# Expert rows added straight into the output, with filling rows written by scatter

## The reference, cut to what matters

```python
x = L0_attn_x                                  # (2, 1024, 512)
xn = _layernorm(x, axis=-1)
x = x + attention(xn, w_attn, b_attn, w_proj, b_proj) + experts(xn, gate_w, w1, w2)
# experts: top 2 of softmax(xn @ gate_w.T), weights divided by their sum
topw, sel = jax.lax.top_k(probs, TOP_K)
act = jax.nn.silu(g) * u                       # g, u: halves of x @ w1[e].T
out = jnp.einsum('eth,te->th', act @ w2[e].T, combine)
```

## Time and profile before

| | us |
|---|---|
| median of three runs | 886.06 |
| the profiled execution | 894.05 |
| its span, first to last instruction | 892.3 |
| PE, DVE, ACT, POOL busy | 809.3, 542.7, 400.9, 256.0 |
| `project_qkv`, up to the first instruction of the next block | 0 to 177.8 |
| `attend` | 177.8 to 553.75 |
| `experts` | 553.75 to 892.3 |

### The profile page before, as it was taken

The page is one execution under the profiler, slowest core; times in us unless marked ns, Lnnn a source line. Parts: engine busy times, 40 slices in busy tenths (PEclk is TensorE's granted clock), DMA queues, the critical chain, the costliest instruction groups (busy, mean ns, idle before and its releaser), DMA issues. The chain is left out here.

```text
span 892.3 us, 13951 instructions
## 1 busy us (share of the span) xinstructions
PE 809.3 (91%) x4033; PEld 570.1 (64%) x4034; DVE 542.7 (61%) x1369; ACT 400.9 (45%) x790; POOL 256.0 (29%) x314
## 2 busy tenths in 40 slices
PE   3889999659999999999999999889999999999990
PEld 3769989535555455555555456677777777777760
DVE  5993543385466566666666655666666666666640
ACT  3241221103465555555655541355555666666630
POOL 3783000043231423233233153002222223222220
PEclk9899999856899999999999999999999999999995
DMA  9476795894556765577673115845564664643436
GB/s 319 154 236 203 222 289 188 277 231 132 164 152 168 226 147 170 126 225 192 175 184 82 17 43 154 293 122 120 131 167 79 167 167 71 167 71 71 71 43 204
DMA packets 80479, 143.23 MB, mean 161 GB/s; under 512 B 16688, under 2 KB 30512, under 8 KB 80368
## 3 DMA queue, kind: packets, MB, share of 16 engines
q1 hardware_dynamic: 43200, 65.72, 24.1%
q10 hardware_dynamic: 29056, 58.28, 23.7%
q0 software_dynamic: 8176, 18.65, 10.8%
HBM read 81.21 MB, written 61.15 MB: 160 GB/s over the span
## 5 line engine op out<-in xcount | busy, mean ns | idle before, releaser
L1402 ACT ACTIVATE probs<-scores_t 128x512 f32<-128x512 f32 (+3 forms) x384 | 163.8, 492 | 145.1 <-PE scores_t L1552 133.3
L913 DVE TENSOR_TENSOR w_lo<-w,w_hi 128x704 fp32r<-128x704 f32 x156 | 131.5, 884 | 89.1 <-ACT w_hi L827 77.0
L1529 PE MATMUL maxima<-k_stack,q_stack 96*128 96x512 f32 (+3 forms) x384 | 142.2, 390 | 12.4 <-DMA q_stack<-qk_hi 8.8
L1572 PE MATMUL o_acc<-probs,v_ones 128*64 128x512 f32 (+3 forms) x768 | 148.2, 508 | 0.5 <-POOL probs L1347 0.5
L1552 PE MATMUL scores_t<-q_stack,k_stack 98*128 98x512 f32 (+3 forms) x384 | 138.6, 386 | 7.1 <-DMA q_stack<-row_lo 5.1
L1436 DVE TENSOR_REDUCE mx<-maxima 128x1 f32<-128x512 f32 x128 | 88.2, 689 | 88.3 <-PE maxima L1529 88.1
L1432 DVE CUSTOM_DVE_ANT_0 masked_scores<-maxima,mask_m 128x128 f32<-128x128 f32 (+3 forms) x256 | 121.6, 485 | 23.6 <-PE maxima L1529 20.5
L976 PE MATMUL gu<-w_hi,rows_hi 128*128 128x352 f32 x312 | 119.6, 383 | 2.7 <-DVE w_lo L913 2.7
L827 ACT CAST w_hi<-w 128x704 fp32r x156 | 114.1, 784 | 9.3 <-issue 9.3
L1552 PEld LDWEIGHTS scores_t<-q_stack,k_stack 98*128 98x128 f32 x384 | 73.5, 194 | 69.3 <-issue 42.3
L994 PE MATMUL down<-w,hidden_t 128*128 (+1 forms) x234 | 107.9, 597 | 0.8 <-DVE hidden_t L896 0.8
(11 more groups left out here) (180 smaller groups left out, 1236.5 us busy)
## 6 DMA issues: line engine op xcount, KB each, us to landing
w<-in_w_t SPq DMA_DIRECT2D x8, 1408.0 KB, 6.6
routed<-blank_row ACTq DMA_DIRECT2D x20, 514.0 KB, 6.8
rows<-routed ACTq DMA_DIRECT2D x39, 256.0 KB, 3.5
qk_hi<-st_hi SPq DMA_DIRECT2D x32, 256.0 KB, 4.8
qk_lo<-st_lo SPq DMA_DIRECT2D x32, 256.0 KB, 6.1
q_stack<-qk_hi ACTq DMA_DIRECT2D x32, 256.0 KB, 4.0
k_stack<-qk_hi ACTq DMA_DIRECT2D x26, 256.0 KB, 4.9
v_all<-o_t SPq DMA_DIRECT2D x4, 1536.0 KB, 5.7
```

The costliest lines, as they stand in the source:

```text
L913: nc.vector.tensor_tensor(w1_lo[r][:, k, :], w1_rows(slot, k), as_f32(w1_hi[r][:, k, :]), ALU.subtract).then_inc(w1_done, 1)
L1402: nc.scalar.activation(probs[:, k % PR, h, 0:w], scores_t[e % RING][:, 0:w], ACT.Exp).then_inc(exp_done, 1)
L1529: nc.tensor.matmul(mb[at % RING][:, 0:w], q_st[i][0:3 * HD, h, t * P:(t + 1) * P], k_st[i][0:3 * HD, h, c * CH:c * CH + w], start=True, st ...
L1572: last = nc.tensor.matmul(o_acc[c][2 * HD * h:2 * HD * (h + 1), CH - w:CH], v_st[i][:, j, h:h + 2, :].rearrange("p o d -> p (o d)"), probs ...
```

## The change

- `acc` is no longer a buffer of its own but a view of the output tensor. The projection's stores and the accumulating DMAs of the experts go straight into the output, and the two copying DMAs at the end are gone, with their wait. The spare rows of `acc` are gone too, and their clearing.
- A slot without a token must now name a row that exists, and no two slots of one tile may name the same row, since an accumulating DMA would lose one of the two additions. Tiles without any token keep the cleared rows, whose token numbers now are 0 to 127. For the empty slots behind the tokens of an expert's last tile, filling rows are written: zeros, with the numbers of tokens among the first 256 that this expert does not serve. They are sent as 2 x 8 indirect DMAs (`pool_fill`), each like one of the 32 scatters; rows not needed go to spare slots behind the others. DVE computes their slots in 12 small operations of round 6 (`dve_fill_links`), and POOL makes four constants in round 1.
- The 16 are placed on POOL in rounds 10 (2), 12 (2), 14 (5) and behind the rounds (7).
- The tags are loaded by ACT at tile `a` = 3 of the second half's projection and awaited by ACT ahead of the expert tiles, and by POOL.
- POOL unrolls its last three expert tiles instead of one, and in these issues the add ahead of the copy of the next tile's numbers.

```diff
-            sp.wait_ge(cleared, 16 * NCH * CLEARS + 16)
+            sp.wait_ge(cleared, 16 * NCH * CLEARS)
...
-            nc.gpsimd.iota(blank[:, D:D + 1].bitcast(U32), pattern=[[0, 1]], base=T, channel_multiplier=1).then_inc(blank_done, 1)
+            nc.gpsimd.iota(blank[:, D:D + 1].bitcast(U32), pattern=[[0, 1]], base=0, channel_multiplier=1).then_inc(blank_done, 1)
...
-            act.dma_start(scratch["acc"][T:T + P, :], blank[:, 0:D]).then_inc(cleared, 16)
...
+    def pool_fill_consts(pool):
...
+        nc.gpsimd.memset(fill_rows[:], 0.0).then_inc(fill_zero, 1)
...
+    def pool_fill(pool, number):
+        a, e = divmod(number, E)
+        pool.wait_ge(fills_done, 1)
+        pool.indirect_dma_start(out=scratch_rows, out_offset=bass.IndirectOffsetOnAxis(
+            ap=fill_slot[:, a, e:e + 1], axis=0), in_=fill_rows[:, a, :], in_offset=None).then_inc(filled, 16)
...
+    def dve_fill_links(dve):
...
+        link(V.tensor_scalar(last_at[:], upto[:], 1.0, float(P), ALU.subtract, ALU.mult))
+        yield
...
+        link(V.scalar_tensor_tensor(member[:], past_last[:], 0.0, both[:, 0:FILL, :], ALU.is_ge, ALU.mult))
...
+        V.tensor_copy(fill_slot[:], fill_to[:]).then_inc(fills_done, 1)
...
             sp.wait_ge(added, 16 * SLOT_TILES)
-            for b in range(B):
-                sp.dma_start(out[b], scratch["acc"][b * S:(b + 1) * S, :]).then_inc(stored, 16)
-            sp.wait_ge(stored, 16 * B)
...
-                after = i if isinstance(i, int) and i == SLOT_TILES - 1 else i + 1
-                nc.gpsimd.tensor_copy(row_index[:, 1 - r:2 - r], tag_of(after)).then_inc(carried, 1)
+                last = isinstance(i, int) and i >= SLOT_TILES - 3
+                if not last:
+                    nc.gpsimd.tensor_copy(row_index[:, 1 - r:2 - r], tag_of(i + 1)).then_inc(carried, 1)
                 pool.indirect_dma_start(out=scratch["acc"], out_offset=bass.IndirectOffsetOnAxis(
                     ap=row_index[:, r:r + 1].bitcast(U32), axis=0), in_=y[:, r, :], in_offset=None, compute_op=ALU.add).then_inc(added, 16)
+                if last and i + 1 < SLOT_TILES:
+                    nc.gpsimd.tensor_copy(row_index[:, 1 - r:2 - r], tag_of(i + 1)).then_inc(carried, 1)
...
-            run_tiles(pool, tile)
+            run_tiles(pool, tile, 3)
...
+                if a == TAGS_AT:
+                    act.dma_start(tags[:], scratch["routed"][0:SLOT_TILES * P, D:XW].rearrange("(a p) d -> p a d", p=P)).then_inc(tags_in, 16)
...
+            act.wait_ge(tags_in, 16)
             run_tiles(act, tile, 3)
...
-    TAG_ROUND = 14
+    FILLS_IN = {10: 2, 12: 2, 14: 5}
+    LINKS_ROUND = 6
+    LINK_EVERY = 2
...
-                if n == TAG_ROUND:
-                    sp.wait_ge(scattered, 16 * TOPK * NT)
-                    sp.dma_start(keep["tags"][:], scratch["routed"][0:SLOT_TILES * P, D:XW].rearrange("(a p) d -> p a d", p=P)).then_inc(tags_in, 16)
...
+            for number in to_fill:
+                fill(pool, number)
             assert next(sent, None) is None
             scale_span(SPANS - 1)
             pool.wait_ge(scattered, 16 * TOPK * NT)
+            pool.wait_ge(filled, 16 * FILL * E)
...
-        "acc": nc.dram_tensor("acc", [T + P, D], F32).ap(),
+        "acc": out.rearrange("b s d -> (b s) d"),
```

More of the change, by code:

```diff
@@ L44 @@
 CLEAR_TILES = -(-SLOT_TILES // (NCH * CLEARS)) * NCH * CLEARS
+FILL = 2
 EARLY = S // P
@@ L552, in _, with route @@
                         turn(c + 1)
-def route(nc, m, keep, count_banks):
+def route(nc, m, keep, count_banks, scratch_rows):
     rank_ps, total_ps = count_banks
@@ L668, in dve_owners, with per_tile, link @@
         V.tensor_copy(keep["expert_end"][:], ends[:]).then_inc(owners_done, 1)
-    return pool_part, pe_part, dve_part, dve_owners, slots_done, owners_done
+    def dve_fill_links(dve):
+        V = nc.vector
+        n = [0]
+        upto_tile = prefix[(NT.bit_length() - 1) % 2][:, NT // 2:, :]
+        def per_tile(ap):
+            return ap.unsqueeze(1).to_broadcast([P, FILL, E])
+        def link(ins):
+            n[0] += 1
+            ins.then_inc(fill_chain, 1)
+            dve.wait_ge(fill_chain, n[0])
+        link(V.tensor_scalar(last_at[:], upto[:], 1.0, float(P), ALU.subtract, ALU.mult))
+        yield
+        link(V.scalar_tensor_tensor(fill_at[:], base[:], float(P), upto_tile[:, NT - 1, :], ALU.mult, ALU.add))
+        yield
+        link(V.tensor_tensor(past_last[:], place[:, 0:FILL, :], per_tile(last_at[:]), ALU.subtract))
+        yield
+        link(V.scalar_tensor_tensor(member[:], past_last[:], 0.0, both[:, 0:FILL, :], ALU.is_ge, ALU.mult))
+        yield
+        link(V.scalar_tensor_tensor(fill_to[:], past_last[:], 0.0, per_tile(fill_at[:]), ALU.max, ALU.subtract))
+        yield
+        dve.wait_ge(fill_consts, 2)
+        link(V.tensor_tensor(fill_to[:], token[:].unsqueeze(2).to_broadcast([P, FILL, E]), fill_to[:], ALU.subtract))
+        yield
+        link(V.tensor_tensor(fill_end[:], fill_to[:], per_tile(last_at[:]), ALU.subtract))
+        yield
+        link(V.scalar_tensor_tensor(fills[:], fill_end[:], float(P), member[:], ALU.is_lt, ALU.is_gt))
+        yield
+        link(V.tensor_tensor(fill_to[:], fill_to[:], spare[:], ALU.subtract))
+        yield
+        link(V.tensor_tensor(fill_to[:], fill_to[:], fills[:], ALU.mult))
+        yield
+        link(V.tensor_tensor(fill_to[:], fill_to[:], spare[:], ALU.add))
+        yield
+        V.tensor_copy(fill_slot[:], fill_to[:]).then_inc(fills_done, 1)
+    return (pool_part, pe_part, dve_part, dve_owners, slots_done, owners_done,
+            pool_fill_consts, pool_fill, dve_fill_links, filled)
 def experts(nc, keep, scratch, x, b_proj, w1_t, w2_t, out):
@@ L687, in experts @@
         LATE = NT - EARLY
+        TAGS_AT = 3
         res = keep["x_rows"][:, :, 0:D]
@@ L699, in experts @@
         tags = keep["tags"]
+        tags_in = m.sem("tags_in")
         warm = m.sbuf("warm", [P, 1], F32)
@@ L1323, in _ @@
             sent = iter(range(TOPK * NT))
+            to_fill = iter(range(FILL * E))
             pool.wait_ge(slots_done, 1)
@@ L1348, in _ @@
                                                 pattern=[[0, PAIR], [1, P]], channel_multiplier=-1).then_inc(masked, 1)
+                    if k == TPC and n == 1:
+                        fill_consts(pool)
+                    if k == TPC and n in FILLS_IN:
+                        for number in itertools.islice(to_fill, FILLS_IN[n]):
+                            fill(pool, number)
                     if k == TPC + 1 and n % PAIRS == 1 and n > PAIRS:
@@ L1469, in _ @@
                 ahead(slot)
+            links = fill_links(dve)
             for n in range(ROUNDS):
@@ L1472, in _ @@
                     ahead(n * NU + u)
+                    if n == LINKS_ROUND and u % LINK_EVERY == 0:
+                        next(links, None)
                     if u == (NB - 1) * PER - 1 and n % PAIRS == 0 and n:
```

39 lines of the change are left out of this document (30 added, 9 removed).

## The result

The changed kernel took 892.62 us as a median of 9 runs (889.72 to 897.85), the kernel before 887.99 us in 9 runs beside it. The ratio is 1.0054, with a 95% interval of 1.0030 to 1.0079: about 0.5% slower, where 872.7 us was forecast. Timed again it was 893.39 us against 890.2 us, ratio 1.0035 (1.0005 to 1.0064).

The account below looks back on a forecast made before the run. The kernel was taken as bounded by PE's work (busy 809.3 of 892.3 us) plus its standstills, the largest at the end. Terms -15.1 - 1.3 + 0.3 + 1.5 + 1.2 = -13.4 on 886.06 gave 872.7 us, range 870.7 to 875.

Parts of the forecast that it names:

- the tags: Second half's projection: the tags land at 583.5, 1.2 us after ACT arrives at its wait; +1.2 us, from 0 to 3.5.
- the end with the copies and the last tiles: End of the program: removing the output copies gains 15.1 us, reordering POOL's last three tiles 1.3 us.
- the fills behind the rounds: Handover to `experts`: POOL waits for seven fills to land at 554.6, so `experts` begins at 555.3; +1.5 us, 0 to 3.4.
- The copies: End of the program: without the two copies it ends with the last add's landing plus 0.4 us; gain 15.1 us.
- the span ends 0.4 us after: End of the program: the same 0.4 us that followed the last copy's landing would follow the last add's landing.
- POOL's last three tiles: Last two adds: they go out without index copy and gap ahead of them; gain 1.3 us, 0.7 to 1.5.
- Constants, fills and links in the rounds: Rounds: constants and fills lie in POOL's idle time, 0; DVE's 12 links in round 6 cost 0.3 us, 0 to 1.5.
- with the same handover: End of `attend`: the block is left 0.66 us after SP's last issue, and this was also put behind the fills' landing.
- still ahead of SP's last store: Handover: POOL's scaling, started 1.4 us later, ends at 551.8, before SP's last store at 552.58.
- a microsecond or so by which ACT's following stores are held at the queue: Tags term: this hold counted only in its upper bound of 3.5 us, beside a landing at 584.5.
- Rival C: Expert tiles: adds into the output land in 7.1 us, so their chain becomes the bound; 891.7 us, +5.6; chance 0.04.
- The rule of the Trainium skill weighed in the prediction: Tags' load: an engine drains packets of typically 9 to 17 descriptors per queue turn; then the tags cost 0, forecast 871.5.

Follow-up runs that it names:

- kernel 3: Changed kernel with the tags loaded by SP behind the weights of expert 2, awaited by ACT only ahead of an expert tile's first result: 883.7 us, ratio 0.9918 to before.
- kernel 11: Changed kernel with the seven late fills moved ahead of the last eight bias additions and the tags on SP: 878.06 us, ratio 0.9853 to before.
- kernel 12: Changed kernel without any filling DMA, their constants and DVE's 12 links, tags still on ACT: 887.9 us, ratio 0.9968 to before.
- kernel 9: Changed kernel with its nine fills of the rounds in 13 (3) and 14 (6), none in 10 and 12: 894.8 us, ratio 1.0025 to before.
- kernel 2: Changed kernel with all 16 fills in rounds 10 to 14 and none behind the rounds: 895.7 us, ratio 1.0068 to before.
- kernel 8: Changed kernel, fills only in rounds 13, 14 and three ahead of the last bias additions, tags behind ACT's last staging copy: 887.5 us, ratio 0.9954 to before.
- kernel 10: Changed kernel with round fills only in 13 (3) and 14 (6), the other seven ahead of the eight bias additions: 887.5 us, ratio 0.9962 to before.

## Why the prediction was wrong

Three terms of the sum failed, in this order of size: the tags (+1.2, measured +8.1), the end with the copies and the last tiles (-16.4, measured -12.4), and the fills behind the rounds (+1.5, measured +5.3). In all three what was priced was the landing of a DMA, and what was missed was an engine held: ACT at its next issue, and POOL in its DRAIN.

- **The copies, -15.1.** They had that length. The step that failed is "the span ends 0.4 us after" the last landing: what lay under the copies was named as "every other engine idle", but POOL had 3.24 us of leaving its block to do, and these stand alone now. With it, -12.1 in the trace.
- **POOL's last three tiles, -1.3.** Half of it came. At the add before the last, which waits for its `y`, 0.7 us were gained. Behind a landing the last add begins 0.74 us later without a copy in between and 0.77 with one, so nothing was. The end is 10.7 without the copies, 9.8 to 10.4 with the change: -0.3 to -0.9. The prediction had named 0.7 as its lower bound, by another split.
- **Constants, fills and links in the rounds, 0 and +0.3.** Nothing that shows: kernels 3 and 11 keep them all and lose nothing ahead of the last maxima, and kernel 12 is without them and gains no more than its handover. The text asked only whether POOL has time; with 13 to 16 fills in the rounds the time did grow, by 2 to 8 us (estimate above), by a path that is not shown.
- **Seven fills behind the rounds, +1.5; measured +5.3.** The landing was put at 554.6; it came at 552.5 in a trace that is 2.3 us earlier by its last maxima, so where it was put. What was missing are the 4.5 us between the landing and the next block. The step that failed is "with the same handover": the 0.66 us were read from SP, whose DRAIN took 0.37 us; POOL's way out could be seen as the 3.40 us before 553.75 and was not put behind the landing. The 2 us by which the scaling was to end "still ahead of SP's last store" were that way out.
- **The tags, +1.2; measured +8.1.** The working followed the bytes: when they flow, whether they land before ACT's wait. Their start came out right (577.2, in a trace whose `experts` begins 3.2 us later, against 574.3). They landed at 581.2, ahead of ACT's wait, so the 1.2 us fell away; the clash with the weights of expert 2 did not occur, since the held projection put these off to 586.8. The price was in "a microsecond or so by which ACT's following stores are held at the queue": 7.05 us, in front of casts on which PE depends, with the lower clock behind it. Moving the load to SP (kernel 3) took the whole term back. The trace of before could not warn: SP's next issue behind its tags stood waiting for ACT anyway.
- **Rival C** is refuted: 39 adds into the output land after 4.4, 5.7 and 10.0 us (least, median, most), against a median of 5.6, and the stretch between first and last `y` is 272.1 against 272.3.
- **The sum.** +5.3 + 8.1 - 12.4, from the means of two traces of each kernel, is +1.0 us. The runs say +4.8 and +3.2. The 2 to 4 us between stay open: they lie ahead of the last maxima, where chance alone moves a trace by as much. Emptying rounds 10 and 12 or dropping all fills and links did not show them.

The rule of the Trainium skill weighed in the prediction ("DMA: Bandwidth & Descriptors", "Queues, rings and completion order"), on how a DMA engine turns between queues, would not have saved the forecast: it bears on when the pieces move, and the term that failed is the hold of ACT. Nor did the prediction's own argument decide it, since turns of whole packets with like numbers of pieces give equal counts too. Kernel 3 shows what either comes to here: in 586.4 to 587.2 SP's queue moved 395 packets, nearly all pieces of 8 bytes, beside 396 of ACT's, so the small pieces did not pass at a larger share.

## What to carry to other kernels

When something long at the end of a program goes, list what every engine still does under it, leaving the block included; idle in the profile is not the same as done. Of a DMA with thousands of tiny pieces ask first what its engine must issue or compute next, and only then when it lands: give it to an engine with nothing behind it. Where POOL's and DVE's work in one place can be taken apart, do it: beside the bias additions DVE's operations took two to three times as long. And two traces are compared by stretches between instructions that both have, since the rest of a single execution may be 5 us of chance.

## What the runs showed of the hardware that was not expected

- POOL's DRAIN at the end of `attend` and of `experts` grows with the number of indirect DMAs that the block issued: 2.67 us for 32 (before, and without any fills), 3.24 for 39 adds, 3.99 for 48 (every kernel with fills, wherever they stood). That is 83 ns for each, in all 15 traces read here. It did not depend on how long ago the last was: 3.99 us both when it had been issued 7 us earlier (kernel 9) and 47 us earlier (kernel 2). All of these DMAs carry 128 rows, so a price by rows fits as well.
- DVE and POOL slow each other where both work at once at the handover: DVE's 0.69 us operation took 1.66 us beside POOL's bias additions in before, and once 10.23 us (kernel 8); the eight additions took 11.7 us in before, 9.2 in kernels 8 and 10. No run varied this alone.
- The issue of a DMA right behind a load of 4992 pieces of 8 bytes in the same queue took 7.05 us, and 8.38 us in the kernel without fills:

```profile
565.77 8.38 ACTq L961 DMA_DIRECT2D out<-o_t  x1
574.20 0.62 ACT L944 CAST rows_hi<-o_t 128x512 fp32r<-128x512 f32 x1 [9.94 <-issue]
```

  In the trace of after the pieces moved from 577.2 to 579.9, and the hold, from 572.4 on, ended at 579.4. In all seven traces with this load in front of ACT's stores it ended 0.5 us before the last piece had moved, so what keeps the pieces waiting ahead (here 4.8 us, behind a store and beside the weights of expert 1) is part of the price. That the queue has a limited place for pieces would explain it; the length of the load was not varied, so this is argued, not shown.
